# LoRA rows of the gate and up projections in three operands, and the four sums of h blocks made by GpSimd

## The reference

```python
def _lora_linear(x, W, A, B, adapter_indices):
    base = jnp.einsum('bsd,df->bsf', x, W)
    lora = jnp.einsum('bsr,brf->bsf', jnp.einsum('bsd,bdr->bsr', x, A[adapter_indices]), B[adapter_indices])
    return base + lora
gate = _lora_linear(x, Wg, Ag, Bg, idx)
up = _lora_linear(x, Wu, Au, Bu, idx)
h = jax.nn.silu(gate) * up
x = x + _lora_linear(h, Wd, Ad, Bd, idx)
x = x + jnp.einsum('bct,bcd->bdt', x, weights[idx])
```

## Time and profile before

| | |
|---|---|
| median of 3 runs | 1187.9 us (1187.41 to 1190.95) |
| the profiled execution | 1185.85 us, its span 1184.2 us |
| granted TensorE clock | 0.995 of full, so 2.4 GHz |
| instructions in the span | 22189 |

### The profile page before, as it was taken

How to read it: one execution, slowest core, us unless ns; L and a number is a source line. 1 busy time by engine, 2 the same in 40 slices (tenths; PEclk the granted TensorE clock), 3 DMA queues, 4 the chain that set the end, 5 groups by cost and what they waited for, 6 DMA issues and landing times.

```text
span 1184.2 us, 22189 instructions
## 1 busy us (share of the span) xinstructions
PE 1152.3 (97%) x6726; PEld 1026.4 (87%) x6726; DVE 968.9 (82%) x1639; ACT 587.8 (50%) x958; POOL 243.1 (21%) x390
## 2 busy tenths in 40 slices
PE   7899999999999999999999999997999999999998
PEld 5788888888888888888888888887999999999997
DVE  6988898988898988889898999986777667767774
ACT  6555454654454645445465455554444444444442
POOL 3133111123211124311111111112323212321220
PEclk9999999999999999999999999999999999999999
DMA  6485455566555468545558676587777777677771
GB/s 212 140 263 175 139 163 157 177 232 174 161 173 155 134 196 297 178 136 166 155 183 278 177 219 201 160 282 250 266 232 246 244 267 241 233 257 263 250 253 58
DMA packets 147496, 241.05 MB, mean 204 GB/s; under 512 B 21458, under 2 KB 90194, under 8 KB 147250
## 3 DMA queue, kind: packets, MB, share of 16 engines
q1 hardware_dynamic: 124912, 180.94, 48.1%
q0 software_dynamic: 21744, 57.57, 15.3%
q10 hardware_dynamic: 722, 1.13, 0.3%
HBM read 169.30 MB, written 70.25 MB: 202 GB/s over the span
## 4 chain that ended last, share of the span: by engine, by line
PE 82%; DVE 7%; DMA 3%; ACT 3%; issue 3%; SPq 1%; DVEq 0%; ACTq 0%
PE ps L1363 16%; PE ps L1364 16%; PE ps L1365 15%; PE ps L1374 9%; PE ps L1531 7%; PE ps L1533 7%; PE ps L1532 7%; DMA h_raw<-h_dram 3%; PE ps L1392 2%; DVE hl L854 1%; ACT xo_hi L561 1%; ACT hh L561 1%; DVE w_lo L854 1%; DVE xst L865 1%; SPq L194 1%
## 5 line engine op out<-in xcount | busy, mean ns | idle before, releaser
L1363 PE MATMUL ps<-xo_hi,w_hi 128*128 128x512 f32 x882 | 350.0, 397 | 3.8 <-ACT u_s L630 3.1
L1364 PE MATMUL ps<-xo_lo,w_hi 128*128 128x512 f32 x882 | 346.1, 392 | 0.0
L1365 PE MATMUL ps<-xo_hi,w_lo 128*128 128x512 f32 x882 | 343.4, 389 | 0.0
L447 POOL DMA_DIRECT2D h_dram<-hs x128 | 96.2, 756 | 542.3 <-DVE hs L992 274.6
L854 DVE TENSOR_TENSOR hl<-h_raw,hh 128x1024 fp32r<-128x1024 f32 x112 | 136.9, 1223 | 82.8 <-ACT hh L561 81.8
L1365 PEld LDWEIGHTS ps<-xo_hi,w_lo 128*128 128x128 f32 x882 | 165.7, 188 | 36.8
L1363 PEld LDWEIGHTS ps<-xo_hi,w_hi 128*128 128x128 f32 x882 | 166.5, 189 | 33.9 <-ACT u_s L630 5.2
L1364 PEld LDWEIGHTS ps<-xo_lo,w_hi 128*128 128x128 f32 x882 | 166.5, 189 | 25.3
L1374 PEld LDWEIGHTS ps<-t_st,bq 128*128 128x128 f32 x1024 | 156.2, 189 | 22.6 <-issue 2.3
L561 ACT ACTIVATE hh<-h_raw 128x1024 fp32r<-128x1024 f32 x112 | 118.0, 1053 | 114.2 <-DMA h_raw<-h_dram 72.5
L1374 PE MATMUL ps<-t_st,bq 128*128 128x256 f32 x1024 | 162.6, 282 | 1.9 <-DVE t_st L854 1.9
(11 more groups left out here) (160 smaller groups left out, 2333.6 us busy)
## 6 DMA issues: line engine op xcount, KB each, us to landing
h_raw<-h_dram SPq DMA_DIRECT2D x112, 512.0 KB, 5.4
bq_raw<-b_twice SPq DMA_DIRECT2D x512, 64.0 KB, 2.2
h_dram<-hs POOLq DMA_DIRECT2D x128, 256.0 KB, 4.2
raw<-packed SPq DMA_DIRECT2D x58, 512.0 KB, 4.6
h_dram<-h_f SPq DMA_DIRECT2D x96, 256.0 KB, 3.1
ad_raw<-a_d SPq DMA_DIRECT2D x64, 128.0 KB, 2.2
xs<-x POOLq DMA_DIRECT2D x16, 512.0 KB, 4.9
y_out_dram<-xs POOLq DMA_DIRECT2D x30, 256.0 KB, 4.7
```

The lines of the kernel that those rows point to most:

```text
L447: pool.dma_start(h_dram[PPG * g:PPG * (g + 1), op, :, k, :].rearrange("q p t -> p q t"), tile[:, col:col + HALF].rearrange("p (q t) -> p q ...
L1363: pe.matmul(bank, st[0], mv[0], start=start and kk == 0, stop=False, skip_group_check=True)
L1364: pe.matmul(bank, st[0], mv[1], start=False, stop=False, skip_group_check=True)
L1365: m = pe.matmul(bank, st[1], mv[0], start=False, stop=kk == 1, skip_group_check=True)
```

## The change

1. **Three operands.** The B rows of the 8 sequences of a pair now stand in three operands (`PARTS`). Operand 0 takes quad 0 whole: its second two sequences on partitions 32 to 127, three times (high twice, low once), and its first two on 0 to 31. Operand 2 does so for quad 1. Operand 1 has the rest: the first two of quad 0 on partitions 0 to 63 and of quad 1 on 64 to 127. Each operand is one matmul of 128 x 256, written to columns 0, 128 and 256 on of the 512 and added there. `t_st` has matching rows, with zeros in operand 1, so a part of `smask`, `t_mask`, `t_hi`, `t_lo` and `order_a` follows.
2. **Splitting B.** `bq_hi` writes high parts to a tile of its own (`bq_high`, 64 partitions), `bq_lo` subtracts it, and a new `bq_rest` of two ScalarE copies makes the remaining rows. TensorE waits for `bq_rest_done` too. Gathers become 12 a pair in place of 8.
3. **The sums** leave VectorE; GpSimd makes each (lines 474 to 503 of the changed kernel) and sends it.
4. Tiles are moved, and GpSimd's A tables have two buffers.

```diff
-                for part in range(2):
-                    for i in range(2):
-                        q = pair * 2 + i
-                        m = pe.matmul(bank[:, i * QT:(i + 1) * QT], b[:, q, part, c % PIECE, u * P:(u + 1) * P],
-                                      t_st[u][g % 2][:, q * QT:(q + 1) * QT], start=start and part == i == 0,
-                                      stop=part == i == 1, skip_group_check=True)
+                for i in range(PARTS):
+                    m = pe.matmul(bank[:, i * P:i * P + QT], b[:, pair, i, c % PIECE, u * P:(u + 1) * P],
+                                  t_st[g % 2][:, pair, i, u, :], start=start and i == 0, stop=i == PARTS - 1,
+                                  skip_group_check=True)
...
             def bq_hi(n, pair):
-                q = slice(2 * pair, 2 * pair + 2)
                 act.wait_ge(bq_in[pair][n % 2], GATHER * (n // 2 + 1))
-                if n >= 2:
-                    act.wait_ge(p4_done, 2 * n - 2)
-                hi(bq[n % 2][:, q, 0, :, :], bq_raw[n % 2][:, q, 1, :, :]).then_inc(bq_hi_done, 1)
+                act.wait_ge(bq_lo_done, bq_turn(n, pair))
+                hi(bq_high[0:64, :, :, :], bq_raw[n % 2][0:64, pair, 0:PARTS:2, :, :]).then_inc(bq_hi_done, 1)
+
+            def bq_rest(n, pair):
+                hi(bq[n % 2][:, pair, 1, :, :], bq_raw[n % 2][:, pair, 1, :, :])
+                hi(bq[n % 2][64:P, pair, 0:PARTS:2, :, :], bq_raw[n % 2][64:P, pair, 0:PARTS:2, :, :]).then_inc(bq_rest_done, 1)
...
+                hi(t[0:64, pair, 2 * h, :, :], t_f[:, :, :]).then_inc(t_hi_done, 1)
+                hi(t[64:96, pair, 2 * h, :, :], t_f[32:64, :, :])
+                hi(t[64 * h:64 * h + 32, pair, 1, :, side], t_f[0:32, :, c]).then_inc(t_rest_done, 1)
...
                 if more:
                     w_hi_sum(s + 1, 1)
+                bq_rest((s + 1) // 2, s % 2)
...
+                for part, lo, end, count in rows:
+                    sp.dma_start(bq_raw[n % 2][lo:end:2, pair, part, :, :].rearrange("r k c -> r (k c)"),
+                                 b_thrice[piece_of(g, k), bass.ds(slot_numbers[g * SLOTS + b], 1), 0:count]
+                                 .rearrange("a r c -> (a r) c")).then_inc(bq_in[pair][n % 2], 16)
...
                 bq_lo((s + 1) // 2, s % 2)
-                if s % 2 == 0:
-                    make_s1(s // 2 - 1)
-                    make_s2(s // 2 - 1)
-                elif not last:
-                    make_s3(s // 2)
-                    if s >= 3:
-                        make_s4(s // 2 - 1)
...
             def store_s3(n):
+                pool.wait_ge(h1_done, 2 * n + 1)
+                pool.wait_ge(h2_done, 2 * n + 1)
+                if n:
+                    pool.wait_ge(h_stored[HS3], 16 * n)
+                pool.tensor_tensor(hs3[:, :], h_f[0][:, 0:HALF], h_f[0][:, HALF:GT], ALU.subtract).then_inc(hs3_done, 1)
                 pool.wait_ge(hs3_done, n + 1)
                 store_sum(2 * n, HS3, hs3, 0)
```

More of the change, by code:

```diff
@@ L54, with cond_resid_kernel @@
 KIB4 = 4096
[L57 removed]
+def cond_resid_kernel(nc, x, xg, idx, packed, wd, a_gu, b_thrice, a_d, b_d, w1, slot_mask, tok_mask, eye, out):
     ctx = ExitStack()
@@ L95, in cond_resid_kernel @@
[L95 to L98, removed]
+        bq = [at(f"bq{i}", 147456 + i * 16384, [P, 2, PARTS, PIECE, WB], F32R) for i in range(2)]
+        bq_raw = [at(f"bq_raw{i}", 147456 + i * 16384, [P, 2, PARTS, PIECE, WB]) for i in range(2)]
+        bq_high = at("bq_high", 159744, [P, 2, PIECE, WB], F32R)
+        t_st = [at(f"t_st{i}", 176128 + i * 12288, [P, 2, PARTS, 2, QT], F32R) for i in range(2)]
@@ L205, in x_turn, with bq_turn @@
             return 7 * g + X_ORDER[g].index(XOPS[k])
+        def bq_turn(n, pair):
+            return 2 * n + (pair if n == 0 else 1 - pair)
         def piece_of(g, k):
@@ L258, in gather @@
                 g, k = divmod(n, PIECES)
-                sp.dma_start(bq_raw[n % 2][b % QS:P:QS, b // QS, 1, :, :].rearrange("r k c -> r (k c)"),
-                             b_twice[piece_of(g, k), bass.ds(slot_numbers[g * SLOTS + b], 1)].rearrange("a r c -> (a r) c"))\
-                    .then_inc(bq_in[2 * b // SLOTS][n % 2], 16)
+                pair, j = divmod(b, SLOTS // 2)
+                q, two = divmod(j // 2, 2)
+                first = two == (q == 0)
+                own, mid, row = 2 * q, 64 * q + j % 2, j % 2
+                rows = [(own, row, 32, RANK), (1, mid, 64 * q + 64, 2 * RANK)] if first else [(own, 32 + row, P, 3 * RANK)]
+                for part, lo, end, count in rows:
+                    sp.dma_start(bq_raw[n % 2][lo:end:2, pair, part, :, :].rearrange("r k c -> r (k c)"),
+                                 b_thrice[piece_of(g, k), bass.ds(slot_numbers[g * SLOTS + b], 1), 0:count]
+                                 .rearrange("a r c -> (a r) c")).then_inc(bq_in[pair][n % 2], 16)
             def gather_pair(n, pair):
@@ L442, in order_a @@
                 pool.wait_ge(t_done, g * QUADS + q)
-                pool.tensor_copy(aq[0][:, :, :, :], a_raw[0][:, :, :, :].rearrange("p s k r -> p k r s")).then_inc(a_ordered, 1)
+                for i in range(2):
+                    two = 2 * (1 - i if q % 2 == 0 else i)
+                    m = pool.tensor_copy(aq[0][:, :, i, :, :],
+                                         a_raw[g % 2][:, two:two + 2, :, :].rearrange("p s k r -> p k r s"))
+                m.then_inc(a_ordered, 1)
             def store_sum(s, op, tile, col):
@@ L746, in _ @@
             bq_hi(0, 0)
+            bq_rest(0, 0)
             order_a_first(2)
@@ L754, in _ @@
             bq_hi(0, 1)
+            bq_rest(0, 1)
             t_hi(0, 3)
@@ L1168, in x_first @@
                 x_lo(0, XOPS.index(op))
+            for i in range(2):
+                for pair in range(2):
+                    m = dve.memset(t_st[i][:, pair, 1, :, :].bitcast(F32), 0.0)
+            m.then_inc(t_zeroed, 1)
             x_first(B11)
```

166 lines of the change are left out of this document (87 added, 79 removed).

## The result

The changed kernel takes 1245.6 us (median of 4 runs, 1245.13 to 1246.71) against 1188.9: a ratio of 1.0481 (1.0465 to 1.0497). It is 4.8% slower, where no change was forecast and the range ended at 1218. The profiled execution has a span of 1244.1.

The account below looks back on a forecast made before the run. TensorE, busy 97%, was taken to bound the kernel, VectorE next. Terms -30.1 + 7 + 11 + 12 + 4 - 1 = +3 us on 1185.85, with the median 2 above, gave 1191; range 1172 to 1218 (the forecast's own 1180 to 1202).

Parts of the forecast that it names:

- So each costs it about 1.2 - 0.2 = 1.0: VectorE's additions beside GpSimd's sums: each sum costs 1.0 us, an even step's first 0.6; average 1.8 a step against 1.20 removed.
- the discount: The 0.2 us taken off a GpSimd sum's assumed 1.2 to get what it costs VectorE's additions.
- A plain round is 9.25 + 1.8 = 11.05: VectorE's round in a plain gate/up step: 11.05 us, under the 11.18 mean of TensorE's steps, so no loss.
- `x_add`'s 0.60: Extra VectorE work of 0.60 us at c = 8 to 14 but 11, counted among the late steps' extras.
- the weight sums of group 3: In group 3, 1.2 us of weight sums fill VectorE's idle 0.87; the round stays by 11.3, costing nothing.
- Rival 2: GpSimd's sums take 1.4 us or more and VectorE bounds plain steps: 1215 us, chance 0.25.
- 0.1175 a matmul: TensorE's four LoRA blocks a step lose one matmul each: 256 x 0.1175 = -30.1 us.
- the start: At the kernel's start, second masks, more A columns to copy and `bq_rest` lengthen the chain: +4 us.
- waits for u3: TensorE waits for VectorE's u3 late in groups 0 to 2, notably c = 9 and 13; mid-group waits total +11 us.
- on queues not waited for: The gathers, 24 in two steps instead of 16 and half more bytes, stay hidden, each a step ahead of use.
- `bq_rest` in even steps: TensorE's LoRA block behind S3 waits 0.25 us for ScalarE's two added copies in 28 even steps: +7 us.
- the boundaries: At three group boundaries, `bq_rest` ahead of x copies and held-up VectorE work delay TensorE: +4.1 each, +12 us.

Follow-up runs that it names:

- the blank sums: The changed kernel with each of GpSimd's four sums replaced by a memset of the same tile, same waits and stores: 1190.3 us, ratio 1.0017.
- the late ones: The changed kernel with both sums of a step back to back on GpSimd, started after VectorE's last `w_lo`, or u3 at c = 15 and 0: 1200.8 us.
- with x spread: The changed kernel with sums back on VectorE, and the next group's four x loads issued in c = 1, 2, 2 and 3: 1186.6 us.
- the first experiment: The changed kernel with the four sums back on VectorE, GpSimd only storing them: 1193.2 us, ratio 1.0044, where 1175 was expected.

## Why the prediction was wrong

**The mechanism was named rightly; the size of one term put it on the wrong side.** The step that failed is "So each costs it about 1.2 - 0.2 = 1.0; only the first of an even step ... costs 0.6", which made "2.0 in odd steps and 1.6 in even ones". Measured: 2.70 and 2.2, mean 2.45. The first sums are near the forecast (1.10 and 0.7 against 1.0 and 0.6); it is the second sum of each step that costs 1.6 and 1.5 in place of 1.0. A sum lasts 1.28 to 1.39 and not 1.2 (L487, 1.28; L494 and L501, 1.30; L479, 1.39), and the second is not paid at its length less 0.2 but at its length plus 0.2 to 0.4, since its hold begins before its record. I took the discount from one copy that had stood idle before it; for the second sum, behind a store, no row existed, and I carried no upper bound for the loss apart from the duration.

**What hung on it.** "A plain round is 9.25 + 1.8 = 11.05, just under the 11.18 mean": the round is right to 0.02 (9.25 + 2.70 = 11.95 against 11.93 measured), with the true loss it is 11.70, and VectorE is the bound in nearly every step. Then nothing else is hidden either: `x_add`'s 0.60 is paid in full (c = 13 lasts 12.54, a plain odd step 11.93), and the weight sums of group 3, forecast at nothing, make its steps 12.14 (mean of s = 50 to 57) against 11.18 forecast. That is where +11.1 stands for -6. Rival 2 had this mechanism, with its threshold at 1.27 us a sum, but priced it at 1215 because it kept the same discounts.

**Right.** 0.1175 a matmul (0.35 for a block of three); the start, +4 against +4.9; additions with two SBUF inputs held up and PSUM ones not; waits for u3 and for `bq_rest` where they were named. The rule of the Trainium skill that I cited ("SBUF — State Buffer", Who interferes with whom) is borne out by the blank sums and the late ones.

**Wrong and covered up.** In the changed kernel VectorE's round hid two more errors. The gathers "on queues not waited for" cost 6.6 us once VectorE is relieved, and SP's issuing of twelve takes 8.2 to 8.8 us in that stretch, where 7.6 followed from the earlier trace rows. `bq_rest` in even steps is 0.39 and not 0.25: no row stood behind its "0.05 to wake"; in the lines above, TensorE begins 0.15 behind the end of the copies (634.55), which itself is 2.90 and not 2.83 after A12's start. And from c = 3 to 9 a group saves nothing (76.4 and 76.0 us in groups 0 and 1 with x spread, 76.3 before, where 1.7 were to be saved), some 5 us in all, which I put down to the second masks and copies of the A side without having tried it. With 4 for even steps (28 x 0.14) and 1.5 at the boundaries they would make up 17 of the 18 us by which the first experiment missed.

## What to carry to other kernels

Work moved to GpSimd is free for VectorE only where VectorE reads PSUM or stands idle: place it by that, and run its instructions back to back with the stores behind them. Beside additions from SBUF, price it by its whole length, and behind a store at 0.2 to 0.4 us more, not at the instruction it removes from VectorE; here 1.20 us removed cost 2.45. And before relieving an engine, compute its round: at 10.45 of 11.05 us it had nothing to give.

## What was unexpected

A VectorE addition that began up to 0.55 us before a GpSimd sum's recorded start, and would have ended before it, was held up until 0.29 after that sum's end (2.14 us in place of 0.42), where a store stood ahead of the sum. And a slower engine can hide a shortage elsewhere: in the changed kernel the gathers of the same burst landed after some 5 us (465 to 490) and ScalarE never waited for them; only with VectorE relieved did TensorE stand still for 4.1 us and then run at a granted clock of 0.50.
